# A four-layer graph network on one core: the first layer norm moved into the edge counting, and the barrier behind the counting taken out

## What is computed

```python
h = jnp.maximum(_layernorm(x, axis=-1), 0.0)
agg = segment_sum(h[src], dst, num_segments=n)      # sum over incoming edges
cnt = segment_sum(ones, dst, num_segments=n)        # degree of each node
y = agg / maximum(cnt, 1)[:, None] @ W_l.T + b_l + h @ W_r.T
y = batchnorm over the nodes(y) * gamma + beta
x = x + relu(y) + h
```

## Time and profile before

| | us |
|---|---|
| median of 3 runs | 1297.7 (1297.63 to 1298.2) |
| the profiled execution's own time | 1298.53 |
| its span in the profile | 1296.8 |
| TensorE (PE) busy in the span | 1171.2 (90%) |
| VectorE busy | 923.9 (71%) |
| ScalarE busy | 706.4 (54%) |
| GpSimd busy | 65.3 (5%) |

### The profile page before, as it was taken

How to read it: one execution, slowest core, us unless ns; L and a number is a source line. 1 busy time by engine, 2 the same in 40 slices (tenths; PEclk the granted TensorE clock), 3 DMA queues, 4 the chain that set the end, 5 groups by cost and what they waited for, 6 DMA issues and landing times. The chain is left out here.

```text
span 1296.8 us, 16930 instructions
## 1 busy us (share of the span) xinstructions
PE 1171.2 (90%) x5865; PEld 729.6 (56%) x5865; DVE 923.9 (71%) x1679; ACT 706.4 (54%) x886; POOL 65.3 (5%) x115
## 2 busy tenths in 40 slices
PE   3999959997998977979999999979988999999996
PEld 3666635554884534435445444434545777777775
DVE  5999864104646696878988987844117888888885
ACT  1132277202647666148787776631116777777774
POOL 3000042000001100000000000000000000000000
PEclk8999959998999997979999999989998999999999
DMA  4000000003003000203111100000020111110102
GB/s 149 5 1 1 1 1 1 1 1 129 1 1 90 1 1 1 81 23 140 43 43 43 43 23 3 1 0 1 1 48 2 26 26 26 26 26 4 23 1 79
DMA packets 24769, 36.15 MB, mean 28 GB/s; under 512 B 11874, under 2 KB 13204, under 8 KB 24694
## 3 DMA queue, kind: packets, MB, share of 16 engines
q1 hardware_dynamic: 24694, 35.14, 9.1%
HBM read 26.03 MB, written 2.70 MB: 22 GB/s over the span
## 5 line engine op out<-in xcount | busy, mean ns | idle before, releaser
L58 PE MATMUL wide<-arena 125*125 (+7 forms) x2028 | 487.2, 389 | 33.3 <-DVE arena L874 12.7
L58 PEld LDWEIGHTS wide<-arena 125*125 (+4 forms) x2028 | 270.4, 141 | 226.8 <-issue 144.8
L1688 PE MATMUL wide<-arena 125*65 125x512 f32 (+1 forms) x480 | 182.3, 516 | 0.0
L1304 PE MATMUL wide<-ident,arena 125*125 125x125 f32 (+3 forms) x954 | 130.0, 283 | 14.0 <-ACT arena L600 4.7
L723 ACT ACTIVATE arena<-arena,b 125x1250 f32<-125x1250 f32 x80 | 106.7, 1336 | 61.1 <-PE wide L1688 56.9
L1213 DVE TENSOR_TENSOR arena<-wide,arena 125x1250 f32<-125x1250 f32 x80 | 116.7, 1459 | 31.3 <-PE wide L1678 31.3
L1304 PEld LDWEIGHTS wide<-ident,arena 125*125 125x125 f32 (+3 forms) x954 | 114.7, 185 | 24.6 <-issue 10.6
L783 ACT ACTIVATE arena<-wide 125x1000 f16<-125x1000 f32 x80 | 80.8, 1011 | 80.8 <-PE wide L1304 80.8
L1688 PEld LDWEIGHTS wide<-arena 125*65 125x65 f32 x480 | 63.4, 138 | 101.8 <-issue 95.4
L798 ACT ACTIVATE arena<-arena,neg_max,unit 125x1250 f32<-125x1250 f32 x80 | 114.3, 1429 | 10.5 <-DVE neg_max L1292 10.5
L1265 DVE SCALAR_TENSOR_TENSOR arena<-wide,arena 125x1000 f16<-125x1000 f32 x80 | 95.9, 1198 | 33.5 <-ACT arena L783 33.5
(11 more groups left out here) (244 smaller groups left out, 1224.1 us busy)
## 6 DMA issues: line engine op xcount, KB each, us to landing
arena<-rows_kept SPq DMA_DIRECT2D x16, 625.0 KB, 6.1
arena<-arena SPq DMA_DIRECT2D x40, 156.2 KB, 2.9
arena<-in_L_gnn_W SPq DMA_DIRECT2D x3, 1024.0 KB, 7.6
x_nm<-in_x SPq DMA_DIRECT2D x2, 1250.0 KB
out<-x_nm SPq DMA_DIRECT2D x1, 2187.5 KB
arena<-in_L_gnn_W_l SPq DMA_DIRECT2D x1, 1024.0 KB, 5.8
arena<-in_L_gnn_W_r SPq DMA_DIRECT2D x1, 1024.0 KB, 8.3
arena<-in_L_gnn_Wk SPq DMA_DIRECT2D x1, 1024.0 KB, 5.4
```

Of the source, the lines that this page charges most:

```text
L58: mm = pe.matmul(ps[0:rows, lo:hi], lhsT, rhs[:, lo:hi], start=start, stop=stop, skip_group_check=True)
L1304: return pe.transpose(dst, src, ident[0:k, 0:k])
L1688: m = pe.matmul(psW[1][0:VA, lo:hi], v_gat[0:ROWS, t, h, :], ring[n % RINGS][0:ROWS, lo:hi], start=(t == 0), stop=(t == TILES - 1))
```

## The change

- The barrier between counting and aggregation is gone; later barriers move up by one number. The flag has a semaphore, `big_set`, and each engine loads it after its work for block 0.
- Statistics: two tiles' at the head of tiles 1 to 5 of the counting. The aggregates come at the head of tile 6, reciprocal and bias at that of tile 7. ACT makes the root in step 5, and h and upper halves in steps 6, 7 and 8 (three, three and four tiles). h has ten buffers.
- VectorE makes the lower halves right after the counting, seven ahead of the split of the degrees and three behind it.
- The turns of counts: pieces 0 and 1 of tile t-1 behind tile t's first group, piece 2 behind tile t's close. The mask of the last tile is made by VectorE from `cnt_f`.
- The turns of h are interleaved with block 1 of the first aggregation, and VectorE copies them out behind block 0.
- POOL's additions are interleaved with its casts, and POOL takes tiles 1 and 6, in both aggregations.
- The arena is laid out anew for this.

The core of the diff:

```diff
-        h32 = [[region(G + o + 512 * i, [D]) for i in range(n)] for o, n in ((5000, RING), (2048, HEAD_HALF))]
-        hot_src = region(0, [2, CHUNKS, N], BF16)
-        hot_dst = region(G, [2, CHUNKS, 128], BF16)
-        cnt_f = [region(o, [N]) for o in (G + 1400, G + 2650, G + 14400)]
-        iota_h = region(G + 3900, [N], F16)
+        h32 = [[region(G + o + 512 * i, [D]) for i in range(n)] for o, n in ((4760, TILES), (2048, HEAD_HALF))]
+        hot_src = region(13510, [2, CHUNKS, N], BF16)
+        hot_dst = region(5120, [2, CHUNKS, 128], BF16)
+        cnt_f = [region(o, [N]) for o in (11250, G + 14396, G + 15646)]
+        iota_h = region(12500, [N], F16)
...
-        BY_ACT = (0, 1, 2, 3, 4, 6, 7, 8)
-        BY_POOL = (5, 9)
+        BY_ACT = (0, 2, 3, 4, 5, 7, 8, 9)
+        BY_POOL = (1, 6)
...
# POOL
-            phase_end(pool, 1)
-            for t in range(TILES):
-                pool.wait_ge(S["h_made"], t + 1)
-                pool.tensor_tensor(x_nm[0:ROWS, t, :], x_nm[0:ROWS, t, :], h32[0][t % len(h32[0])][0:ROWS, :], ALU.add).then_inc(S["x_plus_h"], 1)
-            widen(0)
+            pool.wait_ge(S["counts_turn_read"], 3 * TILES)
+            for k in range(KD):
+                widen(0, k)
+                for t in range(3 * k, min(3 * k + 3, TILES)):
+                    pool.wait_ge(S["h_made"], t + 1)
+                    pool.tensor_tensor(x_nm[0:ROWS, t, :], x_nm[0:ROWS, t, :], h32[0][t][0:ROWS, :], ALU.add).then_inc(S["x_plus_h"], 1)
...
# ACT
+            def norm_first(*tiles):
+                for t in tiles:
+                    act.activation(h32[0][t][0:ROWS, :], x_nm[0:ROWS, t, :], ACT.Relu, bias=nbias[0:ROWS, t:t + 1],
+                                   scale=rstd[0:ROWS, t:t + 1]).then_inc(S["h_made"], 1)
+                    upper_part(0, t)
+
+            for t in range(TILES):
+                act.wait_ge(S["tile_counted"], t + 1)
+                if t >= 3:
+                    act.wait_ge(S["counts_turning"], 3 * (t - 2))
+                copy(cnt_f[t % 3][0:ROWS, :], psW[t % 2][0:ROWS, 0:N], accum_out=deg_col[0:ROWS, t:t + 1]).then_inc(S["counts_f32"], 1)
+                if t >= 1:
+                    turned_counts(t - 1, 2)
+                if t < TILES - 1:
+                    act.activation(mask[0:ROWS, t, :], ...).then_inc(S["mask_made"], 1)
+                for r in range(2):
+                    turned_counts(t, r)
+                if t == 5:
+                    take_root(ROWS, 0, TILES)
+                if t == 6:
+                    act.wait_ge(S["ln_ready"], 1)
+                if 6 <= t <= 8:
+                    norm_first(*(range(0, 3), range(3, 6), range(6, TILES))[t - 6])
+            turned_counts(TILES - 1, 2)
+            act.wait_ge(S["deg_turned"], 1)
+            copy(row_sb[:, :], psS[0][0:3 * TILES, 0:ROWS]).then_inc(S["deg_row_out"], 1)
...
# ACT's widen, and the same in TensorE's aggregate
+                    if big is None:
+                        act.wait_ge(S["big_set"], 1)
+                        big = has_big_count(act)
...
-            phase_end(act, 1)
-            big = has_big_count(act)
-            relu_norm(0)
-            widen(0, big)
+            big = widen(0)
...
# VectorE
-                if t >= 1:
-                    x_stats(t - 1)
+                if 1 <= t <= HEAD_HALF:
+                    x_stats(2 * t - 2)
+                    s = x_stats(2 * t - 1)
+                if t == HEAD_HALF:
+                    done(s)
+                if t == HEAD_HALF + 1:
+                    ln_begin(0, TILES)
+                if t == HEAD_HALF + 2:
+                    ln_end(0, TILES)
...
+            for t in range(TILES - 3):
+                lower_part(0, t)
             dve.wait_ge(S["counts_f32"], TILES)
             split_cols(...).then_inc(S["deg_split"], 1)
+            for t in range(TILES - 3, TILES):
+                lower_part(0, t)
+            done(ts(mask[0:ROWS, TILES - 1, :], cnt_f[(TILES - 1) % 3][0:ROWS, :], 0.0, BARRED, ALU.is_equal, ALU.mult))
             dve.wait_ge(S["deg_wide"], 1)
-            done(blocks_out(dve.tensor_copy, pos_b, psW[0], 128))
+            done(blocks_out(dve.tensor_copy, pos_b, psW[1], 128))
...
-            phase_end(dve, 1)
-            big = has_big_count(dve)
-            ln_stats(0)
...
+            dve.wait_ge(S["big_set"], 1)
+            big = has_big_count(dve)
             for k in range(KD):
                 counts_of_block(0, k, big)
                 tt(aggT[:, k, :], psW[k % 2][:, 0:N], rdeg_b, ALU.mult).then_inc(S["agg_taken"], 1)
+                if k == 0:
+                    for t in range(TILES):
+                        turned_tile(0, t)
...
# TensorE, counting
                 count_group(t, ends[t], True)
-                if t >= 2:
-                    turn_counts(t - 2, 2)
+                for r in range(2 if t >= 1 else 0):
+                    turn_counts(t - 1, r)
...
-                for r in range(2 if t >= 1 else 0):
-                    turn_counts(t - 1, r)
-            for t in (TILES - 2, TILES - 1):
-                for r in range(2 if t == TILES - 2 else 0, 3):
-                    turn_counts(t, r)
-            pe.wait_ge(S["counts_turn_read"], 3 * TILES)
+                if t >= 1:
+                    turn_counts(t - 1, 2)
+            for r in range(3):
+                turn_counts(TILES - 1, r)
+            pe.wait_ge(S["counts_turn_read"], 3 * TILES - 1)
...
-            phase_end(pe, 1)
...
# TensorE, aggregate
                         tile(k, j, cntT_16[l][(TILES * (l * KD + k) + j) % QUAD], j == 0).then_inc(S["cT_used"], 1)
+                        if l == 0 and k == 1:
+                            turn_h(0, j)
...
-            big = has_big_count(pe)
-            turn_h(0, *range(TILES))
-            aggregate(0, big)
+            pe.wait_ge(S["mask_made"], TILES - 1)
+            big = aggregate(0)
```

More of the change, by code:

```diff
@@ L464, in _, with widen @@
             done = Order(pool, S["pool_done"])
[L466 to L472 removed]
+            def widen(l, k):
+                for j in BY_POOL:
+                    n = TILES * (l * KD + k) + j
+                    after(pool, "cT_used", n - QUAD + 1)
+                    pool.tensor_copy(cntT_16[l][n % QUAD][0:ROWS, :], cntT[0:ROWS, j, :]).then_inc(S["cP_wide"], 1)
             many = dict(allow_small_or_imprecise_dtypes=True, channel_multiplier=0)
@@ L515, in _ @@
                 pool.partition_all_reduce(kmaxa[:, half], kmax[:, half], 128, RMAX).then_inc(S["kmax_all"], 1)
-            phase_end(pool, 2)
-            widen(1)
+            phase_end(pool, 1)
+            for k in range(KD):
+                widen(1, k)
             pool.wait_ge(S["hT_made"], 3 * TILES)
@@ L619, in widen @@
                             copy(cntT_16[l][QUAD][0:ROWS, :], cntT[0:ROWS, j, :]).then_inc(S["lo_wide"], 1)
+                return big
             def log_counts(t):
```

131 lines of the change are left out of this document (49 added, 82 removed).

## The result

The changed kernel took 1278.36 us (median of 4 runs, 1275.47 to 1280.28), the kernel before in the same job 1297.95. The ratio is 0.9839, 95% interval 0.981 to 0.9868. The prediction was 1278.6, with a range of 1274.8 to 1284.5. The profiled execution took 1278.7 with a span of 1277.0.

A forecast was written before the change was run, and what follows sets the result against it. Bound: one chain, with a 32.24 us stretch before the first aggregation where neither TensorE nor VectorE is near full. Minus 26.8, plus 0.8, 0.7 and 6.2 gives minus 19.1: 1298.53 becomes 1279.4, median 1278.6; range 1274.8 to 1284.5.

The forecast's parts named there:

- The long stretch (-26.8): Between counting and first aggregation: layer norm, flag and barrier leave the path, so the aggregation starts 26.8 us sooner.
- The aggregation starts at T + 5.4: First aggregation begins 5.4 us after T, the end of the counting's last close, instead of 32.24 us.
- the rule that I had set aside: Before the aggregation: POOL's first cast locks out VectorE's mask or lower half, up to 1.2 us; time 1279.8; not added.
- The counting (+0.8): Counting of edges: VectorE's added statistics cost 0.8 us, from 0 to 1.5; reordering TensorE's turns changes nothing.
- The flag (+0.7): End of the first aggregation's block 0: loading the flag adds 0.7 us on TensorE, hidden on other engines.
- The turns of h (+6.2): Block 1 of the first aggregation: ten turns of h at about 0.62 us each add 6.2 us.
- Block 0 (13.1): First block of the first aggregation: stays at 13.1 us, partly at half clock; bounds 10.9 and 15.
- rival 2: Pause and block 0: full clock held or regained at once, block 0 10.9 us; 1275.5 to 1276.5 us; chance 0.15.
- VectorE's degree chain, margin 1 us: Block 1's third turn of h: VectorE's first copy is ready 1 us before TensorE asks; stall taken as 0.
- rival 1: Late degree chain, TensorE trailing VectorE in counting, or late ACT tiles return 3 to 8 us: 1282 to 1287; chance 0.12.
- Rival 3: Counting's 196 wide hot writes slow at new addresses; gain gone at 0.10 us more each, 1385 at half pace; chance 0.02.
- Rival 4: Another wait replaces the barrier, so the aggregation starts near 20 us after the last close; 1290 to 1297; chance 0.03.

The follow-up runs named there:

- the run in which POOL waits: Changed kernel with POOL's first cast made to wait for VectorE's last lower half; one run, 1278.72 us.
- the repeat: The changed kernel measured a second time, unedited, beside the improved ones on the same chip; 1279.54 us, ratio 0.9849.
- ACT's sums: Changed kernel with VectorE's loop-bound loads ahead of its waits, POOL's first cast behind the last lower half, and ACT making tiles 0 to 3's statistics; 1272.75 us.
- both: Changed kernel with VectorE's loop-bound loads ahead of its waits and POOL's first cast behind the last lower half; 1274.0 us, ratio 0.9819.
- the old casts: Changed kernel with POOL casting tiles 5 and 9 again instead of 1 and 6, in both aggregations; 1279.93 us, ratio 0.9861.

## Why the prediction was right, and where its steps were not

The total was right, and so was its main term, by its mechanism. That the median came within 0.3 us is in part luck: the terms behind the main one are off by up to 7 us each and cancel. Point by point:

- **The long stretch (-26.8).** Measured -26.2. All of the layer norm lies under the counting, ACT's last four tiles end in time, and the table load (1.28 us at 115.57) is hidden. The half-microsecond is the next point.
- **"The aggregation starts at T + 5.4".** It started at T + 6.07. The chain to the spread was faster than I had it (T + 4.65), being at full clock, and the last lower half later. The step that failed is "by the rows the cast begins at T + 3.6 and the lower halves end at T + 4.1, within the slack": the three halves ran with the cast in their middle and took 2.92 us. With the cast out of the way, twice and in different ways, they took 1.89. The slack was smaller too: the halves end at T + 4.87 without the cast (the run in which POOL waits), not at T + 4.1, which leaves 0.3 us up to the start and not 1.3; and VectorE's degree chain behind them had no slack at all. So for two whole instructions side by side the rule that I had set aside holds: the Trainium skill, "SBUF — State Buffer", section "SBUF: two separate sides", says that such a VectorE operation with two inputs and GpSimd lock each other out for whole instructions, and the runs agree with it: one lower half of 1.71 us instead of 0.69, and 1.1 us at the end of the aggregation. Its time in the prediction, 1279.8, can't be told from mine by these runs. What removing the cast gave is seen in the stages and not in the medians, as what follows the aggregation varies by more.
- **The counting (+0.8).** Measured +0.5, by two errors that cancelled, which is luck. The failed step is "TensorE's turns are the same in number, in another order": the order alone took 6.7 us out, since eight turns cover the load of the loop bound that the earlier trace rows show as 0.68 us of issue. The other is VectorE's extra, put at 0.8 us, from 0 to 1.5, from busy times only; it was 7.2 (123.71 against 116.49). 4.05 of it were loads behind semaphores, which have no busy time. The rest, some 3.2, was not split to the end: it is the second set of statistics a tile in tiles 1 to 5 (leaving half of the sets out gave 1.6), the aggregates, and scale and bias. 1.9 of the 7.2 show as busy time of TensorE (117.88 against 115.98), most of it the half clock behind a gap.
- **The flag (+0.7).** On TensorE nothing was to be seen: the idle time of its weight loads ahead of block 0's close is 0.31 us of issue, as in the kernel before, and the products follow 0.16 us behind the start of the close (0.15 before). The term should have been 0; the load overlaps with products that are already queued. On VectorE the load lies bare, in the gap of 0.91 us ahead of block 0's multiplication; the prediction had it there, with 0.8.
- **The turns of h (+6.2).** Block 1 took 16.1 us against 10.9 for a block with its close: 5.2, of which 0.73 is the stall at the third turn. A turn between products adds 0.45 us, not 0.62; four transposes start 0.16 us before the recorded end of the products ahead of them, and the next products 0.17 before theirs.
- **Block 0 (13.1).** 12.49, between forecast and rival 2: the clock fell 6.3 us behind T, and not 2.8, and was back 3.5 us into the products. In the repeat and the variants in which it fell before or at the start it was 12.15 to 13.32, by where the fall came. For the time it made no difference: the wait of the third turn takes up what block 0 gains.
- **VectorE's degree chain, margin 1 us.** Missed by 0.73. The chain came 0.9 us later than forecast (the copy of the degrees starts at T + 6.72 and not at T + 5.8), about what the cast cost, and TensorE came 0.8 sooner (T + 22.86 without the wait, and not T + 23.7). So the third turn started at T + 23.59, nearly where the forecast had it, but by VectorE's path and not by TensorE's. A small part of rival 1; its other two places (TensorE behind VectorE, ACT behind T) split: the first came true in full and was hidden by the order's gain, the second didn't.
- **Rival 3** is out: 549 ns against 541, 537 to 555 in the other profiles of the same counting, and the same cadence. Rival 4 is out.
- **Behind the aggregation.** 1.2 us of the 21.0 don't arrive in the span. The timeline of layer 1, at its first product of keys, shows one place: eight products that took 1.96 us in the kernel before took 3.62 in the changed one, at half clock, behind a wait of 2.59 where before had 1.31:

```profile
308.51 3.62 PE L1480 MATMUL wide<-arena 128*128 128x256 f32 x8 [2.59 <-DVE arena L920]
```

In the repeat this product took 3.75, with ACT's sums 1.97. But this place alone doesn't explain the missing 1.2 us: with ACT's sums what follows the aggregation took 1059.6 us, more than the 1058.2 of the changed kernel, whose repeat took 1060.9, against 1056.95 in the kernel before. Over the profiles it spans 1056.5 to 1060.9, and the granted clock in its thin stretches differs among them. So 1.2 us is within what this part varies by; its cause was not isolated.

Open: what sets the phase of the clock from run to run, and how much of the spread about a median is due to it; and what the rest of VectorE's cost in the counting is made of. The hot writes took 0.57 to 0.58 us instead of 0.54 in the last 18 us of the counting of the changed kernel, without a change of cadence; in "both" and with the old casts ACT normalizes beside them too, and they took 0.53 to 0.54, so it isn't ACT's traffic as such.

## What to carry to other kernels

Price an order, not only the work in it: look for each "issue" gap in front of a loop or a register load, and put long, independent, already released work just ahead of it; where you can, keep such loads in front of semaphore waits. Busy time doesn't bound what work costs that is moved onto a nearly full engine, since its waits and loads come with it. Before you speed up the start of a stage, look for the next place where two engines meet in it, and for which of them comes last there. When two stages are gained at once, check each against a run with only one part of the change: a total that fits may be two misses.

## What the runs showed of the hardware that was not expected

- Two loads of loop bounds on VectorE cost 1.7 to 1.9 us when they stand behind a semaphore wait, and at most 0.64 when they stand ahead of it. On TensorE the same kind of gap (0.68) vanishes behind 1.04 us of queued transposes.
- Nine dispensable products in a pause of 5 us kept the granted clock at 1.00 throughout in one profile; in the changed kernel, its repeat and the variants with the same pause it fell 3.2 to 6.3 us behind the end of the dense work and was back some 3 to 5 us into the products.
- A VectorE operation of 0.69 us with two inputs took 1.71 beside a POOL cast, and the cast 1.56 instead of 1.23.
- POOL's additions, spread among its casts, took 1.09 us each instead of 1.45, beside other neighbours.
- A row sum on ACT costs a second instruction: 0.19 to 0.20 us behind each 0.63 of the pass.
